# The projection bias of a linear attention: added to x by GpSimd, or by bf16 matmuls in PSUM

## The reference, cut to what matters

```python
x = x + 0.5 * ffn(layernorm(x))        # 16 experts, 2 of them for each token, and a shared one
x = x + attention(layernorm(x))
x = x + 0.5 * ffn(layernorm(x))

def attention(x):                      # 16 heads of 16 features
    q, k, v = split(x @ w_qkv.T)
    q, k = relu(q), relu(k)
    z = 1 / (sum over d of ksum * q + eps)     # ksum: the sum of k over the tokens
    context = v^T k                            # for each head
    return ((context q) * z) @ w_proj.T + b_proj
```

## Time and profile before

| | |
|---|---|
| time, median of 3 runs | 1309.13 us (1305.36 to 1309.68) |
| span of the profiled execution | 1417.3 us, 26677 instructions |
| time of the profiled execution | the page gives its span alone |
| PE busy | 1238.7 us, 87% |
| PEld busy | 982.1 us, 69% |
| DVE busy | 838.3 us, 59% |
| ACT busy | 736.0 us, 52% |
| POOL busy | 696.5 us, 49% |

### The profile page before, as it was taken

The page is one execution under the profiler, slowest core; times in us unless marked ns, Lnnn a source line. Parts: engine busy times, 40 slices in busy tenths (PEclk is TensorE's granted clock), DMA queues, the critical chain, the costliest instruction groups (busy, mean ns, idle before and its releaser), DMA issues.

```text
span 1417.3 us, 26677 instructions
## 1 busy us (share of the span) xinstructions
PE 1238.7 (87%) x6864; PEld 982.1 (69%) x6864; DVE 838.3 (59%) x2756; ACT 736.0 (52%) x1700; POOL 696.5 (49%) x849
## 2 busy tenths in 40 slices
PE   4999879799999994999899999999688999999991
PEld 3556556478888883878787787766445988888750
DVE  4576743345565554677858677676532655555567
ACT  3345431056676664565645543544102767676578
POOL 2456754447877775110320412257460777777740
PEclk9999996899999997999989899999899999999996
DMA  9722221745555443111301300012166555554398
GB/s 350 224 72 76 91 79 61 169 132 153 164 158 157 133 136 105 60 60 60 90 31 61 105 30 31 31 61 87 61 150 245 145 159 150 151 151 142 92 350 361
DMA packets 93800, 181.54 MB, mean 128 GB/s; under 512 B 17464, under 2 KB 60240, under 8 KB 91862
## 3 DMA queue, kind: packets, MB, share of 16 engines
q1 hardware_dynamic: 66342, 110.44, 25.5%
q0 software_dynamic: 26016, 67.55, 13.9%
q10 hardware_dynamic: 1296, 1.86, 0.4%
HBM read 97.63 MB, written 86.08 MB: 130 GB/s over the span
## 4 chain that ended last, share of the span: by engine, by line
PE 51%; DVE 15%; ACT 11%; issue 8%; another core or an unknown queue 7%; POOL 5%; DMA 2%; DVEq 0%; ACTq 0%; POOLq 0%; SPq 0%
PE bank L669 16%; PE bank L679 8%; PE bank L532 6%; PE bank L548 4%; POOL expert_rows L1601 4%; PE bank L660 4%; PE bank L509 3%; PE bank L775 3%; ACT w L965 2%; ACT rows L965 2%; PE bank L725 2%; PE bank L701 1%; DVE rows L1381 1%; DVE stat L1106 1%
## 5 line engine op out<-in xcount | busy, mean ns | idle before, releaser
L1664 POOL DMA_INDIRECT routed_rows<-xn,rdest x286 | 282.5, 988 | 175.5 <-issue 79.8
L669 PE MATMUL bank<-rows,att 128*128 128x128 f32 x2288 | 306.1, 277 | 3.3 <-issue 1.5
L669 PEld LDWEIGHTS bank<-rows,att 128*128 128x128 f32 x2288 | 279.9, 193 | 8.4 <-ACT att L954 4.3
L1601 POOL DMA_INDIRECT expert_rows<-rows,slots x160 | 154.9, 968 | 159.0 <-DVE slots L1158 78.5
L1381 DVE SCALAR_TENSOR_TENSOR rows<-bank,tile_b,att 128x128 f32<-128x128 f32 x286 | 99.8, 349 | 170.3 <-ACT att L959 108.4
L679 PE MATMUL bank<-w,rows 128*128 x572 | 178.5, 394 | 18.8 <-DVE rows L1381 16.9
L954 ACT COPY att<-w 128x512 f32 x286 | 179.7, 628 | 10.3 <-issue 6.5
L959 ACT ACTIVATE att<-bank,tile_b 128x128 f32<-128x128 f32 x286 | 107.2, 375 | 110.5 <-PE bank L669 105.4
L548 PE MATMUL bank<-ws,be 128*128 128x256 f32 x512 | 135.7, 416 | 22.3 <-DVE be L1291 22.3
L1394 DVE TENSOR_TENSOR xn<-bank,be 128x256 f32<-128x256 f32 x286 | 121.6, 425 | 38.6 <-issue 22.7
L548 PEld LDWEIGHTS bank<-ws,be 128*128 128x128 f32 x512 | 103.1, 209 | 49.1 <-DVE be L1291 29.2
(11 more groups left out here) (202 smaller groups left out, 2120.6 us busy)
## 6 DMA issues: line engine op xcount, KB each, us to landing
rows<-expert_rows SPq DMA_DIRECT2D x286, 129.5 KB
rows<-routed_rows SPq DMA_DIRECT2D x32, 512.0 KB
w<-routed_rows SPq DMA_DIRECT2D x10, 1024.0 KB, 10.7
w<-in_w SPq DMA_DIRECT2D x2, 4096.0 KB, 18.3
out<-xres SPq DMA_DIRECT2D x16, 512.0 KB, 9.4
xres<-in_x SPq DMA_DIRECT2D x7, 1024.0 KB, 7.5
rows<-routed_rows SPq DMA_DIRECT2D x6, 1024.0 KB, 8.2
expert_rows<-pad SPq DMA_DIRECT2D x47, 129.5 KB
```

The lines of the kernel that those rows point to most:

```text
L669: last = nc.tensor.matmul(rh_ps[t % RB][:, n * P:(n + 1) * P], m.rw13[:, t % RB, c * C + n * INTER:c * C + (n + 1) * INTER], m.rT[:, t % R ...
L1601: nc.gpsimd.indirect_dma_start(out=d.xg, out_offset=bass.IndirectOffsetOnAxis(ap=m.slots[:, slots_of(r), k, i:i + 1], axis=0), in_=m.xs[bu ...
L1664: nc.gpsimd.indirect_dma_start(out=d.yt, out_offset=bass.IndirectOffsetOnAxis(ap=m.rdest[:, n:n + 1], axis=0), in_=m.ry[:, n, :], in_offse ...
```

## The change

The table of biases is no longer loaded as a whole, split, written to HBM and read back. b_proj is loaded once, copied to all partitions (`b_proj`, 128 x 256, fp32). The bias matmuls go, with their weights `ones3`. In their place POOL adds `b_proj` to x of batch b, 16 pieces of 128x128, after ScalarE has normalised this batch into `xn` (the normalisation must see x without the bias) and before VectorE adds the attention output. In batches 0, 1, 2, 4 and 6 the 16 pieces stand in one block ahead of `a_rstd(b + 1)`; in batches 3, 5 and 7 two pieces stand behind each of the first eight sends. VectorE's `add` waits for the batch's last piece. SP issues the loads of x of batches 1 to 7 and of the expert weights one behind the other.

```diff
+            sp.dma_start(m.b_proj[:], d.biases[BPROJ:BPROJ + C].rearrange("(o c) -> o c", o=1).to_broadcast([P, C])
+                         ).then_inc(s.b_proj_in, 16)
             sp.wait_ge(s.x_first, 16)
-            load_x(1)
-            sp.wait_ge(s.bias_split, 3)
-            sp.dma_start(d.bias_parts.rearrange("k (p f) -> p k f", p=P), bias_p).then_inc(s.bias_bounced, 16)
-            load_x(2)
-            sp.wait_ge(s.bias_bounced, 16)
-            sp.wait_ge(s.rows_zeroed, 1)
-            sp.dma_start(m.bias_rows[0:3, :], d.bias_parts[:, BPROJ:BPROJ + C]).then_inc(s.bias_placed, 16)
-            for b in range(3, BATCHES):
+            for b in range(1, BATCHES):
                 load_x(b)
...
-                        nc.tensor.matmul(out, m.qT_sb[:, p % 2, n * P:(n + 1) * P], m.m_sb[:, c, :],
-                                         start=c == 0, stop=False)
-                    last = nc.tensor.matmul(out, m.ones3[:], m.bias_rows[:], start=False, stop=True)
+                        last = nc.tensor.matmul(out, m.qT_sb[:, p % 2, n * P:(n + 1) * P], m.m_sb[:, c, :],
+                                                start=c == 0, stop=c == KC - 1)
...
             def add(b, p):
+                dve.wait_ge(s.b_proj_added, b + 1)
                 dve.wait_ge(s.ay_ready, PAIRS * b + p + 1)
...
-            nc.vector.memset(m.bias_rows[:, :].bitcast(U32), 0).then_inc(s.rows_zeroed, 1)
-            dve.wait_ge(s.bias_loaded, 16)
-            nc.vector.tensor_copy(bias_p[:, 0], bias_f).then_inc(s.bias_split, 1)
...
+            def add_b_proj(b, parts):
+                for j in parts:
+                    c = j % 2 * P
+                    x = m.xres[:, b, j // 2, c:c + P]
+                    last = nc.gpsimd.tensor_tensor(x, x, m.b_proj[:, c:c + P], ALU.add)
+                    if j == 2 * NT - 1:
+                        last.then_inc(s.b_proj_added, 1)
...
                     send(r, j // NT, j % NT)
+                    if j < NT:
+                        add_b_proj(b, range(2 * j, 2 * j + 2))
...
+            pool.wait_ge(s.b_proj_in, 16)
             for b in range(BATCHES):
                 sent = early_in(b, 2)
+                pool.wait_ge(s.a_xn_half, 2 * b + 2)
                 if sent is not None:
                     early_scatter(sent, b)
                 else:
+                    add_b_proj(b, range(2 * NT))
                     a_rstd(b + 1)
```

More of the change, by code:

```diff
@@ L101, in allocate @@
     m.tile_b13 = sb("tile_b13", [P, 2, TILES])
-    m.bias_rows = sb("bias_rows", [P, C], BF16)
+    m.b_proj = sb("b_proj", [P, C])
     m.be2 = sb("be2", [P, E * C])
@@ L115, in allocate @@
     m.ident = sb("ident", [P, P])
-    m.ones3 = sb("ones3", [P, P], BF16)
     m.ones_b = sb("ones_b", [P, P], BF16)
@@ L307, in program @@
     s.pool_steps, s.dve_steps = sem("pool_steps"), sem("dve_steps")
-    s.bias_loaded, s.bias_split, s.bias_bounced = sem("bias_loaded"), sem("bias_split"), sem("bias_bounced")
-    s.rows_zeroed, s.bias_placed = sem("rows_zeroed"), sem("bias_placed")
+    s.b_proj_in, s.b_proj_added = sem("b_proj_in"), sem("b_proj_added")
     s.x_first, s.first_stats, s.first_rstd, s.first_nmr = (
@@ L427, in _ @@
                          ).then_inc(s.bs2_in, 16)
-            sp.dma_start(bias_f, d.biases.rearrange("(p f) -> p f", p=P)).then_inc(s.bias_loaded, 16)
+            sp.dma_start(m.b_proj[:], d.biases[BPROJ:BPROJ + C].rearrange("(o c) -> o c", o=1).to_broadcast([P, C])
+                         ).then_inc(s.b_proj_in, 16)
             sp.wait_ge(s.x_first, 16)
-            load_x(1)
-            sp.wait_ge(s.bias_split, 3)
-            sp.dma_start(d.bias_parts.rearrange("k (p f) -> p k f", p=P), bias_p).then_inc(s.bias_bounced, 16)
-            load_x(2)
-            sp.wait_ge(s.bias_bounced, 16)
-            sp.wait_ge(s.rows_zeroed, 1)
-            sp.dma_start(m.bias_rows[0:3, :], d.bias_parts[:, BPROJ:BPROJ + C]).then_inc(s.bias_placed, 16)
-            for b in range(3, BATCHES):
+            for b in range(1, BATCHES):
                 load_x(b)
@@ L789, in _ @@
             pe.wait_ge(s.att_weights_in, 16 * len(att_loads))
-            pe.wait_ge(s.bias_placed, 16)
             for n in range(4):
@@ L865, in copy_xT @@
                     act.wait_ge(s.h3_ready, 4 * (r - XS) + 4)
-                elif r == 0:
-                    act.wait_ge(s.bias_bounced, 16)
                 elif r == BATCHES + EARLY:
@@ L1446, in add @@
                 TT(x, x, ay_ps[p % 2][:], ALU.add).then_inc(s.ay_added, 1)
-            nc.vector.memset(m.bias_rows[:, :].bitcast(U32), 0).then_inc(s.rows_zeroed, 1)
-            dve.wait_ge(s.bias_loaded, 16)
-            nc.vector.tensor_copy(bias_p[:, 0], bias_f).then_inc(s.bias_split, 1)
-            dve.wait_ge(s.bias_split, 1)
-            ch.then(TT(bias_r, bias_f, bias_p[:, 0], ALU.subtract))
-            nc.vector.tensor_copy(bias_p[:, 1], bias_r).then_inc(s.bias_split, 1)
-            dve.wait_ge(s.bias_split, 2)
-            ch.then(TT(bias_f, bias_r, bias_p[:, 1], ALU.subtract))
-            nc.vector.tensor_copy(bias_p[:, 2], bias_f).then_inc(s.bias_split, 1)
             ch.did(nc.vector.memset(m.ones_b[:], 1.0))
@@ L1676, in _ @@
             ch.did(nc.gpsimd.memset(m.ident[:], 0.0))
-            ch.did(nc.gpsimd.memset(m.ones3[:], 0.0))
             ch.did(nc.gpsimd.memset(m.before[:], 0.0))
@@ L1691, in _ @@
                                            base=0, pattern=[[-1, P]], channel_multiplier=1))
-            ch.did(nc.gpsimd.affine_select(out=m.ones3[:], in_=m.ones3[:], compare_op=ALU.is_ge, fill=1.0,
-                                           base=-3, pattern=[[0, P]], channel_multiplier=1))
             ch.did(nc.gpsimd.affine_select(out=m.before[:], in_=m.before[:], compare_op=ALU.is_ge, fill=1.0,
@@ L1761, in build @@
     d.yt = nc.dram_tensor("routed_rows", (2 * TOKENS, C), FP32, kind="Internal").ap()
-    d.bias_parts = nc.dram_tensor("bias_parts", (3, NBIAS), BF16, kind="Internal").ap()
     with ExitStack() as ctx:
```

3 lines of the change are left out of this document (removed).

## The result

The changed kernel takes 1322.51 us (median of 4 runs, 1321.94 to 1326.18); the kernel before took 1309.41 us beside it (4 runs, 1305.36 to 1311.14). The ratio is 1.011, with a 95% interval of 1.0088 to 1.0132: slower by 13.1 us between the medians (11.5 to 17.3 by the interval), where 8.3 were forecast. That of the changed kernel does: span 1320.5 us.

What follows compares the result with a forecast made beforehand. The prediction saw PE holding half the last-ending chain, DVE next, both taking turns in attention. Additions lose 15.8 us, PE gains 4.4, the start 3.1: +8.3 on the 1309.13 median gives 1317 us, own range 1311 to 1324, whole 1302 to 1327.

Steps and rivals of the forecast that it cites:

- signs of its being wrong: DVE's L1402, L1403 keeping 0.69 us, additions beyond 0.413 us apart where DVE works, or no PE wait at L733, batches 0, 1, 7.
- Start: First ten microseconds: DVE takes x's statistics without waiting for the biases; 3.1 us gained, ends 0 and 3.1.
- PE: Attention phase: 64 bias matmuls removed from PE; 4.4 us gained, ends 2 and 7.0.
- the 0.66: PE's gain in us per batch: 0.22 each from pairs 0, 2 and 3, nothing from pair 1.
- Batch 0: Block of 16 additions delays DVE's combining of batch 1 by 5.7 us; 4.4 us lost after idle time.
- Batch 1: Block holds up the same DVE work by 5.8 us; 3.4 us lost after idle time and slack.
- rival 1: POOL and DVE alternate, each DVE operation waiting for one addition, 0.37 us; net +2.1, 1311 us; chance 0.20.
- Batches 4 and 6: Block behind the last scatter hits small DVE operations of the expert choice; 1.1 us lost each, ends 0 and 2.5.
- Batches 3 and 5: Two additions behind each of eight scatters: power 5.9 us later but covered; DVE loses 1.0 us each.
- Rival 3: Slower still: POOL's additions also wait for DVE, 3 us more in each of batches 3 and 5; 1323 us; chance 0.15.
- Batch 7: Power behind the fourth scatter 3.0 us late, L1419 meets additions for about 0.6; 3.6 us lost.
- Rival 2: Faster: additions hidden in batches 0 and 1, only batch 7's 3.0 us of scatters remain; 1302 us; chance 0.17.

Runs made afterwards that it cites:

- no_adds: The changed kernel without POOL's 128 additions of b_proj, so the bias is missing in the output; waits kept: 1301.53 us, ratio 0.9952.
- start_only: The kernel before with only the splitting of the bias table moved behind the second batch's statistics; bias matmuls stay on PE: 1304.45 us, ratio 0.9959.
- before_again: The kernel before, unchanged, profiled a second time: 1310.35 us, span 1308.5.
- gapped: The changed kernel with each addition of the projection bias waiting for the one ahead of it: 1330.19 us, ratio 1.0159.
- the memsets: The changed kernel with each of the 128 additions replaced by a POOL memset of 128x256 that waits for the one ahead: 1312.97 us, ratio 1.0041.
- after_again: The changed kernel, unchanged, run again with a second profile beside blocks_again: 1322.13 us, ratio 1.0109.
- after: The changed kernel itself in its first profile, span 1320.5 us: 1322.51 us, ratio 1.011.
- seven_moved: The changed kernel with only batch 7's additions moved behind the first power, four after each of scatters five to eight: 1323.13 us, ratio 1.0131.
- blocks_gapped: The changed kernel with each addition waiting for the one ahead only in the blocks of batches 0, 1, 2, 4, 6: 1317.98 us, ratio 1.0087.
- blocks_again: blocks_gapped run again, unchanged, with a second profile: 1316.03 us, ratio 1.0046.

## Why the prediction was right, and which terms were off

The sign holds, and the mechanism holds in batches 0, 4, 6 and 7: VectorE's operations with two SBUF inputs stand still beside a row of additions, and a power behind additions comes late. In batch 1 it does not. The sum was 4.8 us short, 8.3 against 13.1. By no_adds the additions cost 21.0 against 15.8, and the gains are 6.3 against 7.5; that makes 14.7, since the kernel before took 1.6 us less beside no_adds than beside the changed kernel. That the sum came so near is in part luck: batch 1 was put 3.1 us too high, batches 0, 4 and 6 some 5 too low, and the start is likely too high as well. (By their own numbers the terms of batches 0 and 1 are 4.5 and 3.5, which makes the sum 16.0.) Of what was to show the forecast right, the early statistics (7.23), the late power of batch 7 (3.2 us later against its stage) and PE's order came; L721 comes 6.2 us later in batch 0 and 0.3 in batch 1 where 3 to 5 were named. Two of the signs of its being wrong came too, both in batch 1: additions further apart than 0.413 us where VectorE works, and no wait of PE at L721.

- **Start, 3.1 forecast:** 3.3 by the medians of start_only, but the traces bear out only about half. The term was read from the longer execution; set against before_again the statistics begin 1.4 us sooner and the first transposes 1.0 to 1.7. At the first transpose of the attention phase, 503.9 us in before_again stands against 501.6 to 504.8 in the twelve profiles with the new start, so what arrives there can't be told from the scatter. Whether the loads that are issued sooner took anything from it is not shown.
- **PE, 4.4 forecast:** about 2.8, by the stages. Between start_only and no_adds the stages that end in batches 1, 2 and 6 shrink by 0.5 to 0.7 at equal clocks, those of 3 and 5 by 0.1 and 0.3, that of 7 and what follows by nothing; that of 4, where their clocks differ, is 0.6 shorter in no_adds than in before_again, both at 0.96. So the 0.66 was right where it applies, and so were the two batches with less, but the outputs of batches 6 and 7 gain nothing. With some 1.4 us of the start that makes 4.2 of the 6.3 us; where the rest lies is open, and the interval of no_adds begins at 3.9.
- **Batch 0, 4.4 forecast:** 6.2. DVE's delay is the whole row, as forecast, but one instruction bears it and the others keep 0.69 us; the idle 1.22 us of the earlier trace rows that was to absorb a part is 0.26 in no_adds. It belonged to the longer execution.
- **Batch 1, 3.4 forecast:** 0.3. This step failed: that DVE stands still while POOL keeps its pace. The engines took turns there: POOL's additions stretched to 0.9 us and DVE's operations lost 0.14 to 0.21 each. It is rival 1's mechanism, in this one block.
- **Batch 2, 0.2 forecast:** nothing that can be seen.
- **Batches 4 and 6, 1.1 each (ends 0 and 2.5) forecast:** 2.8 and 2.9 at an equal clock, above the upper end. Small operations were thought to lose about their own count of additions; a single one lost nearly all the rest of the row (5.65 us).
- **Batches 3 and 5, 1.0 each forecast:** 1.1 to 1.6 each; DVE's L1386, L1387 and L1401 take 1.2 to 1.6 us there in place of 0.7. The late power is covered, as forecast. Rival 3's number, 1323, is the measured time, but not by its mechanism: the first additions of VectorE behind that power are not late. Its mechanism appears in gapped, at 15 us.
- **Batch 7, 3.6 forecast:** 3.4, and 1.4 more behind it, which the forecast did not have: at the end of PE's longer wait the clock fell to its lower level, and the 14 us from there have 0.76 in place of 1.00. A spell at 1.2 GHz stands in or right behind this wait in all eight profiles in which it lasts 2.63 to 6.87 us, and in none of the five in which it lasts 0.47 to 1.03.
- **The new wait of DVE, nothing forecast:** nothing (5.05 us idle against 4.99).
- **Operations with one SBUF input, taken as free:** the statistics are (0.41 to 0.43 us each beside the additions), but in batch 7 the addition of epsilon (L1098) took 1.20 us beside a pair of them in place of 0.17.

Rival 2 (hidden) is refuted by no_adds: the additions are anything but free. By the page's rule (the Trainium skill, SBUF — State Buffer, section SBUF: two separate sides), by which who starts first has the ports for one instruction and the other blocks, batch 1 and gapped are as they should be, and so are the memsets (with the wait between them), since the rule binds a two-input VectorE instruction only against a GpSimd instruction that reads. In batch 0 and beside the blocks of 4 and 6 the runs differ from it: VectorE waited for the rest of a whole row, 16 additions and some 14, not for one.

Open: why the row hands over in batch 1 and not in batch 0. In both, the instruction is the same and arrives about 0.1 us after an addition has begun. In after_again it arrives 0.36 us after one in batch 0 and is kept out for 7.65 us all the same, so the moment of its arrival doesn't explain it.

## What to carry to other kernels

Time in which an engine is idle is not free where its work can hold up the engine on the path. Place such additions by what the other engine does beside them, put a pause between them where that one works, and keep them behind, not ahead of, the small instruction that somebody waits for. Before work is moved off an engine, see whether it can be moved ahead of that engine's wait: the same bias products, issued earlier on TensorE, came level with leaving them out (ratio 0.9951 against 0.9952). An idle slot or a wait read from one profiled execution can be counted on only if its span agrees with the timed runs: here the 1.22 us of batch 0 and half of the start's 3.1 us were not there again.

## What the runs showed of the hardware

- A row of GpSimd additions without a pause can keep a VectorE instruction out for all of it: 7.65 to 8.03 us in batch 0, and 5.64 to 5.65 us in six cases of six (two blocks in each of after, after_again and seven_moved). With a pause between all additions (gapped), about 0.53 us from one start to the next instead of 0.413, none lasted over 0.98 us.
- GpSimd's memsets, each waiting for the one ahead of it, did not hold up VectorE's two-input operations at all (0.67 to 0.69 us); a row of them without the wait was not run.
- A scatter behind an addition that is waited for starts 0.84 us after its end, and 0.17 without the wait.
- TensorE's granted clock moves a stage of 42 us by as much as the additions do there: 42.0 to 42.2 us at 1.00 and 45.0 at 0.92 with the same instructions (blocks_gapped, blocks_again), and the stage that has it differs from one execution to the next. The rows say 1.00 or a mix of this, 2.4 GHz, with the level of 1.2 GHz.
